# Four node stages of a graph network: one step of the skew for each handover between engines, wide column sums and a row scale on ACT in layer 1

## The reference, cut to what matters

```python
# layer 0: agg = softmax-weighted sum of v[src] over the edges of a node
gate = sigmoid(concat([skip, agg, skip - agg]) @ Wg + bg)
rst = gate * skip + (1 - gate) * agg
rst = layernorm(rst) * ln_g + ln_b;  rst = where(rst >= 0, rst, a * rst)
x = layernorm(x + rst)                     # and er = (x @ W) . attn_r for layer 1
# layer 1: ft = attention-weighted sums of (x[src] + bond) @ W, two heads
h = ft.mean(axis=heads)
h = (h - h.mean(axis=nodes)) / sqrt(h.var(axis=nodes) + eps) * gamma + beta
x = layernorm(x + relu(h))
# layer 2: agg = softmax-weighted sum of messages
hn = leaky_relu(agg @ W_out) + x
x = layernorm(x + where(deg > 0, layernorm(hn) * gamma + beta, x))
# layer 3: agg = mean of the messages of a node
x = layernorm(x + relu(concat([x, agg]) @ upd_w1 + upd_b1) @ upd_w2 + upd_b2)
```

## Time and profile before

| | us |
|---|---|
| median of 3 runs (9449.11 to 9462.87) | 9455.97 |
| the profiled execution | 9457.62 |
| its span, first to last instruction | 9455.9 |

### The profile page before, as it was taken

One profiled execution on the slowest core, in us unless ns is written; L12 is line 12 of the kernel. 1 busy time (PEld: TensorE's weight loads), 2 busy tenths in 40 slices (PEclk: granted clock), 3 DMA queues, 4 the chain that ended last, 5 costly groups with the idle time before them and its releaser, 6 DMA issues. The chain is left out here.

```text
span 9455.9 us, 67678 instructions
## 1 busy us (share of the span) xinstructions
PE 3076.2 (33%) x16664; PEld 2790.0 (30%) x16664; DVE 4752.6 (50%) x6576; ACT 3294.1 (35%) x4415; POOL 6635.2 (70%) x6983
## 2 busy tenths in 40 slices
PE   4000000000110000000065666666656555555555
PEld 3000000000110000000064666666645555555544
DVE  2165565565657777777724444444455222222223
ACT  2022222222213232232214555555533444444441
POOL 4677777777677777777646777777764777777764
PEclk6555555555555555555557888888865555555555
DMA  8233333333123333333313434443421333333321
GB/s 322 65 106 110 106 105 110 106 107 105 36 63 98 110 110 100 108 110 101 95 37 133 131 126 136 136 134 127 132 67 44 95 95 90 89 95 95 92 88 42
DMA packets 369380, 982.81 MB, mean 104 GB/s; under 512 B 166707, under 2 KB 177614, under 8 KB 354675
## 3 DMA queue, kind: packets, MB, share of 16 engines
q1 hardware_dynamic: 136350, 664.53, 19.0%
q0 software_dynamic: 224640, 290.91, 13.5%
q10 hardware_dynamic: 8276, 26.25, 0.7%
HBM read 582.42 MB, written 398.79 MB: 104 GB/s over the span
## 5 line engine op out<-in xcount | busy, mean ns | idle before, releaser
L754 POOL DMA_INDIRECT qv<-qv_table,edge_ix x1512 | 1426.7, 944 | 484.7 <-issue 484.7
L754 POOL DMA_INDIRECT g<-x_table,edge_ix x1512 | 1426.6, 944 | 483.1 <-issue 480.6
L754 POOL DMA_INDIRECT se<-x_table,edge_ix x1512 | 1427.2, 944 | 460.8 <-issue 460.8
L754 POOL DMA_INDIRECT comb<-x_table,edge_ix x1512 | 1426.6, 944 | 460.8 <-issue 460.8
L825 DVE TENSOR_TENSOR_SCAN edge_val<-edge_bank,edge_val 128x464 f32<-128x464 f32 (+1 forms) x728 | 699.9, 1031 | 1438.2 <-ACT edge_val L1288 1431.6
L1399 PE MATMUL fix_ps<-ident,fix_wide 128*128 128x128 f32 x14 | 4.1, 455 | 4263.6 <-DVE fix_wide L1363 4263.6
L1399 PEld LDWEIGHTS fix_ps<-ident,fix_wide 128*128 128x128 f32 x14 | 3.2, 323 | 4264.6 <-DVE fix_wide L1363 4264.6
L835 ACT ACTIVATE edge_sums<-edge_val 128x1904 f32<-128x1904 f32 (+3 forms) x224 | 1135.2, 5068 | 8.3 <-DVEq L1325 8.3
L810 ACT ACTIVATE edge_bank<-edge_weight_arg 128x112 f32<-128x112 f32 (+2 forms) x168 | 38.4, 229 | 2220.0 <-DVE edge_decay_arg L804 2220.0
L1259 PE MATMUL h_ps<-w_hidden,edge_comb_t 97*128 97x128 f32 x3136 | 741.6, 420 | 19.7 <-ACT edge_val L1288 19.0
L825 DVE TENSOR_TENSOR_SCAN edge_val<-edge_decay,edge_val 128x493 f32<-128x493 f32 (+1 forms) x672 | 714.0, 1131 | 13.4
(11 more groups left out here) (329 smaller groups left out, 8722.3 us busy)
## 6 DMA issues: line engine op xcount, KB each, us to landing
sums<-edge_sums SPq DMA_DIRECT2D x56, 1848.0 KB
sums<-edge_sums SPq DMA_DIRECT2D x56, 1792.0 KB, 7.1
sums<-edge_sums SPq DMA_DIRECT2D x56, 1008.0 KB
sums<-edge_sums SPq DMA_DIRECT2D x56, 924.0 KB, 3.8
edge_k<-k_edges SPq DMA_DIRECT2D x56, 896.0 KB
edge_bond<-in_edge_attr SPq DMA_DIRECT2D x56, 896.0 KB
edge_eh<-in_edge_attr SPq DMA_DIRECT2D x56, 896.0 KB
edge_qr<-in_edge_attr_n SPq DMA_DIRECT2D x56, 896.0 KB
```

Source lines behind the costliest of these rows:

```text
L754: e.indirect_dma_start(self.gather_into(b, j), None, self.gather_from, bass.IndirectOffsetOnAxis(ap=now[:, j:j + 1], axis=0))\
```

## The change

`in_turn` now takes pairs of a lag and a stage function, so that a lag can be chosen. In all four node stages each function that waited for another engine in its middle is cut at that wait, and its halves stand at least one step apart: turn, move, multiply and the use of the result are four entries. DVE's list keeps its order, with larger lags behind a product. In layer 1 the seven pairs of sum products become one pair of 448 columns each, over seven partial sums that DVE folds at the end, and the scaling of rows moves from DVE to ACT, as one ACTIVATE a column (98 of them), while the reciprocal stays on DVE.

```diff
-def in_turn(groups, *stages):
-    for step in range(groups + len(stages) - 1):
-        for k in reversed(range(len(stages))):
-            if 0 <= step - k < groups:
-                stages[k](step - k)
+    for step in range(groups + max(lag for lag, _ in stages)):
+        for lag, stage in reversed(stages):
+            if 0 <= step - lag < groups:
+                stage(step - lag)
 # layer 0, PE
-            for g in range(groups):
-                times_attn.turn(e, g, p.x[:, ph.now(g), :])
-                times_attn.multiply(e, g, p.attn_r)
+            in_turn(groups,
+                    (6, lambda g: times_attn.turn(e, g, p.x[:, ph.now(g), :])),
+                    (7, lambda g: times_attn.multiply(e, g, p.attn_r)))
 # layer 0, ACT (lags 0 to 4 as before)
-                    take_er)
+                    (6, lambda g: times_attn.move(e, g)),
+                    (7, take_er))
 # layer 1, PE
             def product(g):
-                times_w.turn(e, g, agg[g % ring])
                 times_w.multiply(e, g, p.w1_heads)
...
-                for t in range(G):
-                    start, stop = g + t == 0, g == groups - 1 and t == G - 1
-                    e.matmul(sum_ps[:, 0:FD], p.ones[:, :], p.aux[:, g * G + t, :], start=start, stop=stop)
-                    last = e.matmul(sum_sq_ps[:, 0:FD], p.ones[:, :], square[g % ring][:, t, :],
-                                    start=start, stop=stop)
-                last.then_inc(summed, 1)
-            in_turn(groups, product, lambda g: None, add_up)
+                e.matmul(sum_ps[:, 0:G * FD], p.ones[:, :], flat(p.aux[:, ph.now(g), :]), start=start, stop=stop)
+                e.matmul(sum_sq_ps[:, 0:G * FD], p.ones[:, :], flat(square[g % ring][:, :, :]),
+                         start=start, stop=stop).then_inc(summed, 1)
+            in_turn(groups,
+                    (1, lambda g: times_w.turn(e, g, agg[g % ring])),
+                    (2, product),
+                    (4, add_up))
 # layer 1, ACT
-            in_turn(groups, lambda g: times_w.move(e, g), square_up)
+            in_turn(groups, (1, lambda g: times_w.move(e, g)), (3, square_up))
...
-            in_turn(len(parts), square_part, root_part)
+            def scale_part(k):
+                e.wait_ge(turned_over, k + 1)
+                for t in range(parts[k].start, parts[k].stop):
+                    x = p.x[:, t, :]
+                    e.activation(x, x, ACT.Copy, scale=ph.var[:, t:t + 1])
+                e.drain().then_inc(ph.finished, 1)
+            in_turn(len(parts), (0, square_part), (1, root_part), (2, scale_part))
 # layer 1, DVE
-            in_turn(groups, aggregate, shift)
+            in_turn(groups, (0, aggregate), (3, shift))
...
+            for k, bank in enumerate((sum_ps, sum_sq_ps)):
+                e.tensor_reduce(sums[:, k, :], bank[:, 0:G * FD].rearrange("p (t f) -> p f t", t=G), AX.X, ALU.add)
...
-            def finish(k):
-                s = parts[k]
+            def turn_over(k):
+                root = ph.var[:, parts[k]]
                 e.wait_ge(from_root, k + 1)
-                scale_rows(e, p.x[:, s, :], ph.var[:, s])
-                e.drain().then_inc(ph.finished, 1)
+                e.reciprocal(root, root).then_inc(turned_over, 1)
 # layer 2, PE
-            in_turn(groups, product, *[lambda g: None] * 4, next_product)
+            in_turn(groups,
+                    (1, lambda g: times_w.turn(e, g, agg[:, ph.now(g), :])),
+                    (2, lambda g: times_w.multiply(e, g, p.w2_out)),
+                    (8, lambda g: times_next.turn(e, g, p.x[:, ph.now(g), :])),
+                    (9, lambda g: times_next.multiply(e, g, p.w3_ux)))
 # layer 2, ACT: move 1, take 2, the Norms 3 to 6, next move 8, take_next 9
 # layer 2, DVE: aggregate 0, add_x 3, sum 4, affine 5, sum 6, finish 7
 # layer 3, PE
-            for step in range(groups + 1):
-                if step < groups:
-                    times_w.turn(e, step, ph.rows[:, ph.now(step), :])
-                if step >= 1:
-                    times_out.turn(e, step - 1, hidden[:, ph.now(step - 1), :])
-                if step < groups:
-                    times_w.multiply(e, step, w_joint)
-                if step >= 1:
-                    times_out.multiply(e, step - 1, p.w3_upd2)
+            in_turn(groups,
+                    (1, lambda g: times_w.turn(e, g, ph.rows[:, ph.now(g), :])),
+                    (2, lambda g: times_w.multiply(e, g, w_joint)),
+                    (4, lambda g: times_out.turn(e, g, hidden[:, ph.now(g), :])),
+                    (5, lambda g: times_out.multiply(e, g, p.w3_upd2)))
 # layer 3, ACT: move 1, out-move 4, square 6, root 7 (before 0 to 3)
 # layer 3, DVE: mean_hidden 0, join 3, residual 6, sum 7, finish 8 (before 0 to 4)
```

More of the change, by code:

```diff
@@ L1695, in _ @@
             in_turn(groups,
[L1696 to L1700, removed]
+                    (0, aggregate),
+                    (1, mix),
+                    (2, lambda g: first.sum_squares(e, g)),
+                    (3, activate),
+                    (4, lambda g: second.sum_squares(e, g)),
+                    (5, finish))
 def node_phase_1(p):
@@ L1724, in node_phase_1 @@
         to_root, from_root = ph.sem("to_root"), ph.sem("from_root")
+        turned_over = ph.sem("turned_over")
+        sums = ph.sb("sums", [P, 2, FD])
         cuts = [0, 25, 50, 74, T]
@@ L1891, in _ @@
         def _(e):
[L1892 to L1897, removed]
-                    e.wait_ge(ones_in, 1)
-                times_next.turn(e, g, p.x[:, ph.now(g), :])
-                times_next.multiply(e, g, p.w3_ux)
-            in_turn(groups, product, *[lambda g: None] * 4, next_product)
+            e.wait_ge(ones_in, 1)
+            in_turn(groups,
[3 more added lines that the diff above has]
+                    (9, lambda g: times_next.multiply(e, g, p.w3_ux)))
         @block.scalar
@@ L1915, in _ @@
             in_turn(groups,
-                    take,
-                    lambda g: first.act_square(e, g, other[:, ph.now(g), :]),
-                    lambda g: first.act_root(e, g, p.eps[:, 1:2]),
-                    lambda g: second.act_square(e, g, p.x[:, ph.now(g), :]),
-                    lambda g: second.act_root(e, g, p.eps[:, 0:1]),
-                    take_next)
+                    (1, lambda g: times_w.move(e, g)),
+                    (2, take),
+                    (3, lambda g: first.act_square(e, g, other[:, ph.now(g), :])),
+                    (4, lambda g: first.act_root(e, g, p.eps[:, 1:2])),
+                    (5, lambda g: second.act_square(e, g, p.x[:, ph.now(g), :])),
+                    (6, lambda g: second.act_root(e, g, p.eps[:, 0:1])),
+                    (8, lambda g: times_next.move(e, g)),
+                    (9, take_next))
         @block.vector
@@ L1967, in _ @@
             in_turn(groups,
-                    aggregate, add_x,
-                    lambda g: first.sum_squares(e, g),
-                    affine,
-                    lambda g: second.sum_squares(e, g),
-                    finish)
+                    (0, aggregate),
+                    (3, add_x),
+                    (4, lambda g: first.sum_squares(e, g)),
+                    (5, affine),
+                    (6, lambda g: second.sum_squares(e, g)),
+                    (7, finish))
 def node_phase_3(p):
@@ L2021, in _ @@
             in_turn(groups,
[L2022 to L2025 removed]
+                    (1, lambda g: times_w.move(e, g)),
+                    (4, lambda g: times_out.move(e, g, ACT.Relu)),
+                    (6, lambda g: norm.act_square(e, g, p.x[:, ph.now(g), :])),
+                    (7, lambda g: norm.act_root(e, g, p.eps[:, 0:1])))
         @block.vector
@@ L2064, in finish @@
                 e.drain().then_inc(ph.finished, 1)
-            in_turn(groups, mean_hidden, join, residual, lambda g: norm.sum_squares(e, g), finish)
+            in_turn(groups,
+                    (0, mean_hidden),
+                    (3, join),
+                    (6, residual),
+                    (7, lambda g: norm.sum_squares(e, g)),
+                    (8, finish))
 def gnn_program(nc, ins, out, n_nodes):
```

30 lines of the change are left out of this document (13 added, 17 removed).

## The result

The kernel after takes 9364.35 us (median of 4 runs, 9362.75 to 9365.62) against 9454.75 (4 runs, 9449.11 to 9462.87): ratio 0.9904, 95% interval 0.9886 to 0.9921. 9377 was forecast, with a range of 9353 to 9405. The profiled execution took 9363.88 us, span 9362.1, so its span is 93.8 us shorter.

| node stage | before | after | measured | forecast |
|---|---|---|---|---|
| layer 0 | 281.1 | 281.8 | +0.7 | 0 |
| layer 1 | 250.2 | 212.7 | -37.5 | -34.5 |
| layer 2 | 217.7 | 228.4 | +10.7 | +10.2 |
| layer 3 | 230.7 | 165.5 | -65.2 | -56.6 |

The account below looks back on a forecast made before the run. Bounds: layer 3 by DVE and PE waiting on each other, layer 1's first half by PE, layer 2 by DVE, layer 0 by POOL. Terms -56.6 - 38.8 + 4.3 + 10.2 = -80.9 give 9377 us, range 9353 to 9405.

Parts of the forecast that it names:

- row scale: Layer 1's end: DVE loses four scale operations (-3.8), the stretch behind the last apply grows (+8.1), together +4.3 us.
- three signs of being wrong: L2058 waiting for PE in every group, a wide product costing twice L548's column, or the gathers' mean above 1.1 us.
- the ring: Layer 3 before: DVE and PE each wait for the other, neither being the bound, 15.0 us a step.
- B: Layer 3: PE keeps a wait of 1.9 us a step for ACT, step 10.9, total 9396 us; chance 0.11.
- the growth of the gathers: Layer 3: gathers lengthened by DVE work beside them, 3.7 us added, giving steps of 9.5 us.
- C: Layer 1: wide products cost as much a column as narrow ones, +34 us, total 9411 us; chance 0.07.
- rival A: Layer 3: PE is granted 2.4 GHz, saving 8 us of the tail, total 9369 us; chance 0.13.
- the forecast's low bound: Layer 1's scale on ACT: by the line through L1550 and L1551 64 elements take 0.21 us, giving -3.
- the waits of the fill: Layer 2's start: DVE's waits for gathers are 23.5 us in all, part of a +8.1 us loss.
- The closest is group 10: Layer 0: POOL's sends keep 3.4 us of cover behind ACT's last square there, so the stage changes by 0.
- D: All node stages: each DVE operation shuts POOL out for its whole length, total 9496 us; chance 0.03.
- E: The skew does nothing; only layer 1's sums gain and added steps cost layer 3, total 9493 us; chance 0.02.

Follow-up runs that it names:

- the second chip: Unchanged kernels after and before run once more on another chip of the forecast's kind: 9381.88 us against 9470.22, ratio 0.9908.
- fifth experiment: Kernel after with layer 1's sums in 28 narrow instructions a group again, new order kept: layer 1 takes 335.3 us against 256.6.
- sixth experiments: Kernel after with layer 1's first half in its old order, wide sums kept: layer 1 takes 293.1 us against 256.6.
- third: Kernel after with layer 1's last row scale on DVE again: layer 1 takes 251.6 us, 4.4 to 5.7 less; ratio to the kernel before 0.9864.
- seventh experiments: Kernel after with layer 1's row scale shared, parts 0 and 1 on ACT, 2 and 3 on DVE: layer 1 takes 249.4 us against 256.6.
- the second: Kernel after with layer 2's node stage in its old order: 12082.04 us, ratio to the kernel before 0.9865.
- eighth experiments: Kernel after with layer 2's first path in old lags, only the second product cut in two steps: layer 2 takes 312.6 us against 310.2 to 312.1.

## Why the prediction was right

The span got 93.8 us shorter, 80.9 were forecast. The 12.9 between are -8.6 in layer 3, -4.1 in layer 1's first half, +1.1 in its row scale, +0.5 in layer 2, +0.7 in layer 0 and -2.5 in the edge stages, which the sum left out. The two large ones have the same sign, so the total does not owe its place in the range to misses that cancel. None of the three signs of being wrong came; the gathers' mean in layer 3 is 0.97 us.

**Layer 3 (-65.2, forecast -56.6).** The mechanism held in each step: the ring is gone, POOL sets the pace, PE keeps no wait of 1.9 us a step (1.3 us in all in the six steps from 9268 to 9322, so B falls), and the tail is 30.1 for 30.9. Mis-sized is the growth of the gathers: "I add 3.7 us for that". They got 3.4 shorter, and 2.8 on the second chip (98.08 to 95.25). With that the steps are 8.96, not 9.5, and the last rows are in 125.9 us behind the stage's start, not 133.3: 7.4 of the 8.6. I had read the longer mean of layer 3 as DVE work beside the gathers; DVE did more of it and the mean fell, so that reading was wrong. What made them long before stays open, and no experiment was made on it.

**Layer 1, first half (-42.9, forecast -38.8).** The gathers became the bound, with rows in at 4885.8; wide products cost L548's price (C falls, by 1.49 us for two passes). The missed 4.1 us are the clock in the tail: rival A's mechanism, in the layer where I held it excluded because "layer 1's PE, nine tenths busy, stays at 0.50". In the fifth experiment, too, 104 busy us of 104 stayed at 0.50 with narrow products, so a busy share was the wrong thing to argue from. The fifth and sixth experiments part the order from the wide products, but on the other kind of chip; on that of the forecast the two were only measured together.

**Row scale (+5.4, forecast +4.3).** The tail is +7.2 for +8.1, mostly by the smaller pitch. But DVE's removed work gave 1.8 us, not 3.8. The sums of parts 1 and 2 after, and that of part 1 before:

```profile
4926.20 1.82 DVE L1868 TENSOR_REDUCE node_var<-node_squares 128x25 f32<-128x1600 f32 x1 [1.20 <-ACT node_squares L1784]
...
4938.84 1.75 DVE L1868 TENSOR_REDUCE node_var<-node_squares 128x24 f32<-128x1536 f32 x1 [0.79 <-ACT node_squares L1784]
```
```profile
4969.69 1.82 DVE L1854 TENSOR_REDUCE node_var<-node_squares 128x25 f32<-128x1600 f32 x1 [0.17 <-issue]
```

With the scale gone from between, DVE waits 1.20 and 0.79 us for ACT's squares, where it had gaps of 0.17: a wait that the scale had covered. (Part 0 waits 1.63 us in both kernels.) In the forecast's low bound, 0.60 and 0.48 give 0.18 for 64 elements, not 0.21, which the unrounded means do; the bound moves by under 2 us. The third and seventh experiments confirm the sign and both sizes.

**Layer 2 (+10.7, forecast +10.2).** The waits of the fill are 24.8 for 23.5, and the sum is repeated on the second chip (+10.2). The split is a little off both ways, +9.4 and +1.3 for +8.1 and +2.1. The cause rests on the waits of the trace, since the second and eighth experiments ran where it is hidden; there they show that the old lags take the waits away, but not what that is worth.

**Layer 0 (+0.7, forecast 0).** "The closest is group 10" was wrong. The profile puts 2.6 us of POOL's waits down to ACT, in four places:

```profile
POOL er_edges L1601 <- ACTq L1631: 2.6, 4, 1.7
```

Three of them are 0.30, no more than the issue gap before every send. The fourth, 1.7, is at group 8. Its cover could be read in the kernel before, from ACT's last square ahead of it and POOL's first send of the group:

```profile
2641.14 0.58 ACT L1489 ACTIVATE node_square<-node_agg 128x448 f32<-128x448 f32 x1 [2.24 <-DVEq L1513]
```
```profile
2642.47 0.98 POOL L1601 DMA_INDIRECT er_edges<-node_er,start_ix  x1 [0.30 <-issue]
```

That is 0.8 us, where group 10 has 3.4.

Of the other rivals, A did not come in layer 3 (clock 0.50), D falls by gathers that did not grow, E by layer 3.

## What to carry to other kernels

Where two engines each wait for the other all through a stage, as DVE and PE did in layer 3, giving each handover its own step takes the stage to its slowest engine; count then the ramp: every added step delays the first groups, and in a stage that one engine's work already bound that was all it did (layer 2, +10.7 us). Read what an operation covers before moving it to an idle engine: the tail behind the last producer decides, not the sum of busy time. Fewer and wider products can be worth more than the time of their columns: in layer 1, on the other kind of chip, 3.0 us a step by the products and 3.6 by the clock.

## What the runs showed of the hardware

- PE at 1.2 GHz in 104.00 busy us of 104 with 64-column products, but at a granted 0.93 in 40.04 busy us of 41 once the sums are 448 columns wide; the same multiply took 3.19 and 1.67 us.
- The kernel before took 9455 us in the first comparison and 9470 on chip 2, but 12241 to 12457 on the three other chips. There a node stage's first groups wait up to 53 us on PE and 58 on ACT without a releaser, after which instructions come at distances of 0.7 to 2.8 us for a while. POOL's gathers run on meanwhile, 92.5 to 97.2 us for 98. What holds the other engines is not known; no run tested it.
